# Other hand-written orders of each engine's work in a four-batch attention kernel

## What is computed

```
def _L0_xattn_ref(x, weight):             # x: layernorm(x), weight: ctx
    xq = quant_dequant_act_1x128(x)       # fp8, one scale per row and 128 columns
    wq = quant_dequant_weight_128x128(weight)   # fp8, one scale per 128x128 block
    return einsum('emk,enk->emn', xq, wq)

def _L0_ffn_ref(x, Wa, Wp, w_std, w_rec):
    fused = x @ (Wa * col_scale)
    Qf, Kf, V = ...                       # 16 heads of 32
    scores = einsum('bhtd,bhsd->bhts', Qf, Kf) / sqrt(32)
    attn = softmax(where(causal, scores, min))
    y = einsum('bhts,bhsd->bhtd', attn, V)
    return y.reshape(Bx, Tx, C) @ Wp

x = x + tanh(g_xattn) * _L0_xattn_ref(_layernorm(x), ctx)
x = x + tanh(g_ffn) * _L0_ffn_ref(_layernorm(x), Wa, Wp, w_std, w_rec)
```

## Time and profile before

| | us |
|---|---|
| median of three runs | 499.98 (499.82 to 503.68) |
| the profiled execution | 499.74 |
| its span, first to last instruction | 497.9 |
| around the span | 1.84 |

### The profile page before, as it was taken

One profiled execution on the slowest core, in us unless ns is written; L12 is line 12 of the kernel. 1 busy time (PEld: TensorE's weight loads), 2 busy tenths in 40 slices (PEclk: granted clock), 3 DMA queues, 4 the chain that ended last, 5 costly groups with the idle time before them and its releaser, 6 DMA issues.

```text
span 497.9 us, 7913 instructions
## 1 busy us (share of the span) xinstructions
PE 440.6 (88%) x2536; PEld 317.1 (64%) x2536; DVE 340.3 (68%) x1122; ACT 255.7 (51%) x498; POOL 151.1 (30%) x278
## 2 busy tenths in 40 slices
PE   0375989998979999998969999999879999999996
PEld 0352767775536788775535788776545788776764
DVE  5999627889994254889995253789995246556633
ACT  1695356566646450667645642466654424554530
POOL 5678474343225200343213400243122101121110
PEclk9998799999989999999999999999998999999999
DMA  7402173323500346223500234424400243234102
GB/s 225 197 1 87 39 246 82 91 69 96 146 2 2 89 101 193 67 56 95 141 27 0 64 97 127 138 53 98 97 11 2 58 102 97 64 95 102 60 21 86
DMA packets 27929, 42.62 MB, mean 86 GB/s; under 512 B 8272, under 2 KB 8528, under 8 KB 27888
## 3 DMA queue, kind: packets, MB, share of 16 engines
q1 hardware_dynamic: 25872, 41.18, 29.6%
q10 hardware_dynamic: 1824, 0.54, 0.6%
q0 software_dynamic: 192, 0.39, 0.3%
HBM read 12.59 MB, written 4.19 MB: 34 GB/s over the span
## 4 chain that ended last, share of the span: by engine, by line
PE 66%; DVE 24%; ACT 3%; issue 3%; DMA 2%; POOL 1%; SPq 0%; ACTq 0%; DVEq 0%; POOLq 0%
PE pv_bank L748 13%; DVE x_all L1201 10%; PE mm_bank L594 9%; PE mm_bank L595 8%; PE mm_bank L596 8%; PE exp_bank L734 6%; PE max_bank L717 5%; DVE max_bank L1230 5%; PE mm_bank L775 2%; PE mm_bank L777 2%; PE mm_bank L776 2%; PE turn_bank L610 2%; DVE bn L1208 2%; PE pv_bank L757 1%; DMA x_all<-in_x 1%
## 5 line engine op out<-in xcount | busy, mean ns | idle before, releaser
L1230 DVE CUSTOM_DVE_ANT_0 max_bank<-max_bank,causal 128x512 f32<-128x512 f32 (+3 forms) x256 | 121.0, 512 | 52.5 <-PE max_bank L717 52.0
L1002 ACT ACTIVATE work<-exp_bank 128x512 f32<-128x512 f32 (+1 forms) x192 | 94.9, 526 | 56.2 <-PE exp_bank L734 55.2
L512 POOL TENSOR_SCALAR_AFFINE_SELECT work<-work 128x384 f32<-128x384 f32 x64 | 33.4, 522 | 281.6 <-ACT work L1002 281.6
L748 PE MATMUL pv_bank<-work,v_aug 128*33 128x256 f32 (+3 forms) x512 | 78.9, 451 | 0.6 <-DVE work L1241 0.2
L734 PE MATMUL exp_bank<-q_stack,k_stack 97*128 97x512 f32 (+3 forms) x256 | 71.2, 341 | 7.6 <-ACT work L1002 6.5
L717 PE MATMUL max_bank<-k_stack,q_stack 96*128 96x512 f32 (+3 forms) x256 | 71.1, 338 | 2.4 <-DVE row_max L1230 1.8
L1201 DVE SCALAR_TENSOR_TENSOR x_all<-mm_bank,coef,x_all 128x128 f32<-128x128 f32 x224 | 61.5, 342 | 0.3
L748 PEld LDWEIGHTS pv_bank<-work,v_aug 128*33 128x33 f32 x512 | 29.7, 113 | 50.1 <-issue 42.1
L734 PEld LDWEIGHTS exp_bank<-q_stack,k_stack 97*128 97x128 f32 x256 | 45.6, 188 | 23.4 <-ACT work L1002 14.7
L594 PE MATMUL mm_bank<-xt_hi,w_hi 128*128 128x512 f32 x128 | 53.4, 417 | 0.7 <-ACT v_aug L981 0.7
L717 PEld LDWEIGHTS max_bank<-k_stack,q_stack 96*128 96x128 f32 x256 | 45.2, 191 | 12.7 <-DVE row_max L1230 3.7
(11 more groups left out here) (168 smaller groups left out, 789.1 us busy)
## 6 DMA issues: line engine op xcount, KB each, us to landing
q_stack<-qk_hi SPq DMA_DIRECT2D x128, 64.0 KB, 2.0
k_stack<-qk_hi SPq DMA_DIRECT2D x120, 64.0 KB, 2.0
x_all<-in_x SPq DMA_DIRECT2D x16, 256.0 KB, 3.6
ctx_raw<-in_ctx SPq DMA_DIRECT2D x16, 256.0 KB, 3.9
q_stack<-qk_lo SPq DMA_DIRECT2D x64, 64.0 KB, 2.0
out<-x_all SPq DMA_DIRECT2D x16, 256.0 KB, 2.4
k_stack<-qk_lo SPq DMA_DIRECT2D x60, 64.0 KB, 2.0
work<-in_L_ffn_Wa SPq DMA_DIRECT2D x3, 768.0 KB, 9.7
```

The costliest lines, as they stand in the source:

```text
L512: pool.affine_select(out=three, in_=three, compare_op=ALU.is_ge, fill=0.0, base=0, pattern=[[0, 3], [1, P]], channel_multiplier=-1)
L748: last = pe.matmul(pv_bank[64 * j:64 * j + D + 1, P * m:T], v_aug[:, m, 2 * u + j, :], prob[j][:, PROB_COL[m]:PROB_COL[m] + T - P * m], st ...
L1002: act.activation(prob[j][:, UNIT_COL[k]:UNIT_COL[k] + UNIT_LEN[k]], exp_bank[(3 * j + k) % 2][:, 0:UNIT_LEN[k]], ACT.Exp, scale=SCALE).the ...
L1230: last = dve.tensor_tensor_reduce(max_bank[unit % 2][:, col:col + width], max_bank[unit % 2][:, col:col + width], causal[:, T - width:T], ...
```

## The change

The strings are written anew for the eight steps of the middle batches (used by batches 0 to 2), for the last batch, for the prologue and for the end sections; nothing else is changed, neither an operation, nor a buffer, nor the table BEFORE. The block sums now stand as S0 to S6, S7 to S11, S12 to S15 in steps 3, 4 and 5 of DVE (before S0 to S4, S5 to S9, S10 to S15). The block maxima of ctx (t) stand in steps 4 and 5, all ahead of the last maxima of step 5. The quarters of q0, k0, q1, k1 are divided otherwise between step 7 and the end section. The norm stands behind back at the end of steps 3 to 5, and W, X, x, u, b and H pieces stand at other places.

```diff
--- before.py
+++ after.py
@@ -38,105 +38,105 @@
 
 
 PE_STEPS = [
-    "max0 max1 rowmax W0 Q2.0 max2 v3.012 exp0 max3 exp1 W1 exp2 Q2.1 exp3 max4 v3.3 exp4 max5 exp5",
-    "Q2.2 max0 max1 rowmax Q2.3 pv exp0 exp1 max2 max3 W2 K2.0 max4 exp2 K2.1 exp3 back K2.2 max5 exp4 exp5 W3",
-    "max0 K2.3 max1 rowmax Q3.0 pv exp0 Q3.1 max2 Q3.2 exp1 max3 max4 back exp2 Q3.3 K3.0 exp3 K3.1 exp4 K3.23 exp5 max5 X0",
-    "max0 rowmax max1 S0 S1 pv max2 S2 max3 X1 max4 exp0 S3 back S4 exp1 exp2 S5 S6 max5 X2 exp3 exp4 exp5",
-    "rowmax max0 max1 S7 pv max2 max3 S8 S9 exp0 max4 exp1 back exp2 exp3 exp4 max5 X3 exp5 S10",
-    "S11 max0 rowmax max1 pv S12 max2 S13 max3 H0 S14 exp0 exp1 max4 exp2 H1 exp3 exp4 S15 exp5 max5 back",
-    "max0 rowmax max1 A0 pv exp0 H2 max2 exp1 exp2 max3 max4 exp3 exp4 max5 exp5 back",
-    "A1 rowmax H3 pv q0.0 exp0 exp1 q0.12 back exp2 q0.3 k0.0 exp3 k0.123 exp4 q1.012 exp5 q1.3 k1.012",
+    "max0 max1 rowmax W0 Q2.0 v3.01 max2 exp0 exp1 max3 v3.2 max4 exp2 exp3 Q2.1 max5 v3.3 exp4 exp5",
+    "max0 max1 Q2.23 W1 rowmax pv K2.0 exp0 exp1 W2 max2 max3 back exp2 K2.1 exp3 exp4 max4 max5 K2.23 exp5",
+    "max0 rowmax Q3.0 max1 W3 pv Q3.12 exp0 exp1 Q3.3 max2 max3 K3.0 exp2 max4 exp3 K3.12 back exp4 exp5 K3.3 max5",
+    "X0 max0 rowmax max1 S0 S1 pv S2 S3 max2 max3 exp0 X1 max4 exp1 S4 exp2 S5 exp3 max5 exp4 exp5 back",
+    "X2 max0 S6 rowmax max1 S7 max2 pv S8 exp0 max3 exp1 S9 exp2 max4 exp3 S10 exp4 S11 X3 exp5 max5 back",
+    "max0 H0 rowmax S12 max1 pv S13 max2 exp0 exp1 max3 S14 exp2 max4 exp3 S15 exp4 H1 max5 exp5 back",
+    "max0 max1 A0 rowmax pv exp0 exp1 max2 H2 exp2 max3 exp3 max4 exp4 max5 exp5 back H3",
+    "rowmax A1 pv q0.01 exp0 q0.2 exp1 q0.3 exp2 k0.0 exp3 exp4 back k0.12 exp5 k0.3 q1.0",
 ]
 
 ACT_STEPS = [
-    "neg W0 exp0 exp1 exp2 W1 exp3 exp4 exp5 v3",
-    "neg Q2 exp0 exp1 copy exp2 W2 exp3 exp4 exp5",
-    "K2 neg W3 copy exp0 C0 exp1 Q3 exp2 exp3 exp4 K3 exp5 X0",
-    "neg C1 copy X1 C2 exp0 exp1 exp2 exp3 exp4 exp5",
-    "neg X2 copy C3 exp0 exp1 exp2 exp3 exp4 exp5",
-    "X3 neg N0 N1 H0 exp0 copy exp1 exp2 H1 exp3 exp4 exp5",
-    "neg N2 N3 exp0 H2 exp1 exp2 copy exp3 exp4 exp5",
-    "H3 neg exp0 copy exp1 c0 exp2 q0 exp3 k0 exp4 exp5 c1",
+    "neg W0 exp0 exp1 exp2 exp3 exp4 exp5 v3",
+    "Q2 neg W1 copy exp0 exp1 exp2 exp3 exp4 W2 exp5 K2",
+    "neg C0 exp0 copy exp1 Q3 exp2 W3 exp3 exp4 exp5 K3",
+    "X0 neg C1 C2 exp0 X1 copy exp1 exp2 exp3 X2 exp4 exp5",
+    "neg C3 exp0 exp1 exp2 exp3 copy N0 exp4 exp5 X3",
+    "H0 neg exp0 copy exp1 N1 exp2 exp3 exp4 exp5 H1",
+    "neg N2 N3 exp0 exp1 H2 exp2 exp3 copy exp4 exp5",
+    "H3 neg exp0 copy exp1 exp2 q0 exp3 exp4 c0 exp5",
 ]
 
 DVE_STEPS = [
-    "max0 max1 max2 max3 x0 x1 max4 max5 x2",
-    "x3 max0 max1 L0 Q2 max2 max3 m0 max4 L1 norm max5 L2",
-    "m1 L3 max0 e0 K2 max1 max2 m2 m3 e1 norm max3 max4 Q3 max5",
-    "K3 max0 max1 S0 S1 max2 max3 S2 S3 S4 norm max4 max5",
-    "b0 S5 max0 S6 S7 max1 b1 max2 S8 max3 max4 S9 norm max5",
-    "S10 max0 max1 S11 t0 S12 max2 max3 H0 S13 max4 S14 b2 S15 t1 t2 max5 t3 norm b3 H1",
-    "A0 max0 max1 max2 max3 max4 max5 H2 norm",
-    "H3 A1 norm q0 k0 q1",
+    "max0 max1 max2 max3 max4 x0 max5",
+    "x1 x2 x3 Q2 max0 max1 L0 m0 L1 max2 max3 m1 max4 max5 norm L2",
+    "e0 max0 K2 L3 max1 m2 m3 max2 max3 max4 Q3 e1 norm max5",
+    "K3 max0 S0 S1 max1 S2 max2 S3 max3 S4 max4 S5 norm max5 S6",
+    "max0 max1 b0 S7 max2 b1 S8 S9 max3 S10 max4 norm t0 max5 S11",
+    "H0 S12 max0 t1 max1 t2 t3 b2 max2 S13 S14 max3 max4 S15 max5 norm b3",
+    "A0 max0 max1 H1 max2 max3 H2 max4 max5 norm H3",
+    "A1 norm q0",
 ]
 
 POOL_STEPS = [
     "zero0 zero1 i0",
-    "zero0 zero1 u0 u1",
     "zero0 zero1",
-    "u2 u3 zero0 zero1",
-    "zero0 zero1 r0",
+    "u0 u1 zero0 u2 zero1",
+    "zero0 zero1 u3",
+    "r0 zero0 zero1",
     "zero0 zero1",
-    "r1 zero0 zero1 g0 g1",
-    "g2 g3 zero0 zero1",
+    "r1 zero0 zero1",
+    "g0 g1 zero0 g2 zero1 g3",
 ]
 
 PE_LAST = [
-    "max0 rowmax max1 Q2.01 v3.01 max2 exp0 exp1 v3.2 max3 exp2 max4 v3.3 exp3 exp4 Q2.2 max5 exp5",
-    "max0 Q2.3 rowmax K2.01 max1 max2 pv exp0 exp1 K2.23 max3 exp2 max4 exp3 back exp4 Q3.0 max5 exp5",
-    "max0 Q3.1 rowmax max1 max2 pv max3 exp0 exp1 Q3.2 back exp2 max4 exp3 Q3.3 exp4 max5 exp5 K3.0",
-    "max0 K3.1 rowmax max1 pv max2 exp0 max3 exp1 K3.2 exp2 back max4 exp3 K3.3 exp4 max5 exp5",
-    "Y0 max0 max1 rowmax Y1 pv exp0 max2 exp1 max3 z0 Y2 exp2 exp3 back exp4 max4 exp5 max5 Y3",
-    "max0 rowmax max1 pv max2 exp0 exp1 max3 max4 back exp2 exp3 max5 z1 exp4 exp5",
-    "Y4 rowmax max0 max1 pv max2 max3 exp0 exp1 Y5 exp2 max4 back max5 exp3 exp4 Y6 exp5 Z0",
-    "rowmax z2 pv exp0 exp1 Y7 exp2 exp3 back exp4 exp5",
+    "max0 max1 rowmax Q2.0 v3.01 Q2.1 max2 exp0 exp1 max3 v3.2 exp2 v3.3 exp3 max4 exp4 max5 Q2.2 exp5",
+    "Q2.3 rowmax K2.0 max0 max1 pv exp0 K2.1 exp1 max2 max3 exp2 K2.2 exp3 max4 K2.3 exp4 max5 exp5 Q3.0 back",
+    "rowmax max0 Q3.1 max1 pv exp0 max2 exp1 max3 Q3.2 exp2 max4 back exp3 max5 exp4 Q3.3 exp5",
+    "K3.0 max0 rowmax K3.1 max1 pv max2 exp0 exp1 K3.2 max3 back exp2 max4 exp3 K3.3 exp4 max5 exp5",
+    "Y0 max0 rowmax z0 max1 pv exp0 exp1 Y1 exp2 max2 max3 back exp3 exp4 max4 Y2 max5 exp5",
+    "Y3 rowmax max0 max1 pv max2 exp0 max3 exp1 z1 back exp2 exp3 max4 max5 exp4 exp5 Y4",
+    "rowmax max0 max1 pv max2 exp0 max3 exp1 Y5 exp2 exp3 max4 max5 back exp4 exp5",
+    "Y6 rowmax Z0 pv exp0 exp1 Y7 exp2 exp3 z2 back exp4 exp5 Z1",
 ]
 
 ACT_LAST = [
-    "neg exp0 exp1 exp2 exp3 exp4 v3 exp5",
-    "Q2 neg exp0 exp1 copy exp2 exp3 K2 exp4 exp5",
-    "neg copy exp0 exp1 exp2 exp3 exp4 exp5 Q3",
-    "neg copy exp0 exp1 exp2 exp3 exp4 K3 exp5",
-    "neg copy exp0 z0 exp1 exp2 exp3 exp4 exp5",
-    "neg copy exp0 exp1 exp2 exp3 exp4 exp5",
-    "neg z1 exp0 exp1 copy exp2 exp3 exp4 exp5",
-    "neg copy exp0 exp1 exp2 exp3 exp4 z2 exp5",
+    "neg exp0 exp1 exp2 exp3 exp4 v3 exp5 Q2",
+    "neg exp0 copy exp1 exp2 exp3 exp4 exp5",
+    "K2 neg exp0 copy exp1 exp2 exp3 exp4 exp5",
+    "neg Q3 copy exp0 exp1 exp2 exp3 K3 exp4 exp5",
+    "neg copy exp0 exp1 z0 exp2 exp3 exp4 exp5",
+    "neg copy exp0 exp1 exp2 exp3 exp4 exp5 z1",
+    "neg exp0 exp1 copy exp2 exp3 exp4 exp5",
+    "neg exp0 exp1 copy exp2 exp3 exp4 exp5",
 ]
 
 DVE_LAST = [
     "max0 max1 max2 max3 max4 max5",
-    "max0 Q2 max1 max2 max3 max4 norm max5",
-    "max0 K2 max1 max2 max3 norm max4 max5",
-    "max0 max1 max2 max3 Q3 max4 norm max5 K3",
-    "Y1 max0 max1 max2 max3 z0 norm max4 max5",
-    "max0 max1 Y3 max2 max3 norm max4 max5",
-    "max0 max1 max2 max3 Y5 z1 max4 max5 norm Y7 Z0",
-    "norm",
+    "Q2 max0 max1 max2 max3 max4 max5 norm K2",
+    "max0 max1 max2 max3 max4 max5 norm",
+    "max0 max1 max2 Q3 max3 max4 max5 norm K3",
+    "max0 max1 max2 max3 max4 max5 norm",
+    "max0 max1 z0 max2 Y1 max3 norm max4 max5",
+    "Y3 max0 max1 max2 max3 z1 Y5 max4 max5 norm",
+    "Y7 Z0 norm",
 ]
 
-PE_FIRST = ("f0 f1 f2 f3 f4 S0 S1 S2 S3 f5 S4 S5 S6 f6 S7 S8 f7 S9 f8 S10 S11 S12 S13 S14 "
+PE_FIRST = ("f0 f1 f2 f3 f4 S0 S1 S2 f5 S3 S4 S5 S6 f6 S7 S8 S9 f7 S10 S11 S12 f8 S13 S14 "
      "S15 f9 f10 v0 f11 v1 q0 B0 B1 k0 V2 q1 M0 k1 M1 M2")
 
-ACT_FIRST = ("a0 C0 C1 C2 f0 d0 f1 C3 f2 C4 b0 f3 f4 C5 C6 f5 a1 C7 f6 b1 f7 N0 f8 a2 "
-     "a3 N1 f9 N2 b2 f10 N3 b3 v0 f11 v1 q0 k0 c0 V2 D0 c1 p0 q1 D1 k1 c2 c3")
-
-DVE_FIRST = ("x0 w0 x1 x2 x3 t0 t1 L0 L1 t2 t3 L2 A0 A1 T0 F0 F1 L3 F2 F3 T1 T2 c0 S0 "
-     "S1 S2 S3 b0 S4 S5 S6 S7 S8 b1 S9 S10 S11 S12 b2 S13 h0 S14 S15 b3 T3 h1 u0 u1 "
-     "h2 u2 h3 u3 B0 q0 B1 k0 M0 q1 M1 M2 k1")
-
-POOL_FIRST = ("i0 s0 s1 s2 s3 s4 s5 o0 s6 j0 s7 r0 j1 l0 l1 r1 l2 l3 r2 r3 j2 j3 g0 g1 "
+ACT_FIRST = ("a0 C0 d0 C1 C2 f0 C3 f1 C4 f2 f3 f4 C5 a1 f5 C6 C7 b0 b1 f6 N0 a2 f7 a3 "
+     "b2 f8 N1 N2 f9 b3 N3 v0 f10 f11 q0 p0 k0 v1 c0 V2 D0 c1 q1 D1 c2 k1 c3")
+
+DVE_FIRST = ("x0 x1 x2 x3 w0 t0 t1 L0 t2 t3 L1 A0 T0 A1 F0 T1 F1 L2 L3 F2 F3 c0 T2 S0 "
+     "S1 S2 S3 S4 S5 b0 S6 S7 S8 b1 S9 S10 T3 S11 b2 S12 h0 S13 S14 S15 b3 u0 h1 h2 "
+     "u1 h3 u2 u3 B0 B1 q0 k0 q1 M0 M1 M2 k1")
+
+POOL_FIRST = ("i0 s0 s1 s2 s3 s4 s5 s6 l0 s7 l1 r0 o0 j0 r1 j1 l2 r2 l3 r3 j2 j3 g0 g1 "
      "D0 g2 D1 g3 p0")
 
-PE_END = "pv k1.3 V0.012 max0 back V0.3 max1 V1.01 y0 max2 y1 V1.2 max3 V1.3 V2.0 max4 V2.123 max5 y2 y3 O0 O1 O2 O3"
-
-ACT_END = "q1 k1 copy V0 y0 V1 y1 c2 V2 y2 c3 y3"
-
-DVE_END = "k1 norm max0 max1 max2 max3 y0 max4 y1 max5 y2 O0 y3 O1 O2 O3"
+PE_END = "q1.123 k1 pv V0.01 max0 back V0.23 y0 V1.0 max1 V1.1 max2 V1.2 max3 V1.3 y1 max4 V2 max5 y2 y3 O0 O1 O2 O3"
+
+ACT_END = "k0 c1 q1 c2 copy k1 y0 c3 V0 V1 y1 V2 y2 y3"
+
+DVE_END = "k0 q1 k1 norm max0 max1 y0 max2 max3 max4 y1 max5 y2 y3 O0 O1 O2 O3"
 
 END_LAST = {
-    "PE": "Z1 Z2 pv Z3 back Z4 Z5 z3 Z6 Z7 Z8 Z9 Z10 Z11",
-    "ACT": "copy z3",
-    "DVE": "z2 Z1 Z2 norm Z3 z3 Z8 Z9 Z10 Z11",
+    "PE": "Z2 pv Z3 back Z4 Z5 z3 Z6 Z7 Z8 Z9 Z10 Z11",
+    "ACT": "z2 copy z3",
```

(1 more changed line is left out.)

## The result

The changed kernel takes 504.79 us (median of 19 runs, 502.63 to 508.07), the kernel before 500.70 beside it (19 runs). The ratio of the runs is 1.0064, with a 95% interval of 1.0049 to 1.0079: slower by about 3.2 us. The sign and the range held. The reasons held only in part, and the main term was not in the sum. The time lies at the lower end of what the forecast gave to another cause (norms that wait for back, 503 to 508, chance .22), which did not happen.

A forecast was written before the change was run, and what follows sets the result against it. A batch was taken as PE-bound, then DVE-bound for 34 us, then PE-bound again. Terms: 499.74 - 2.9 (stretch) + 1.2 (clock) + .75 (scales) + 2.0 (step 0) = 500.79, median 501.0 us; range 495.5 to 506.

The forecast's parts named there:

- The sign and the range: Whole kernel: forecast 1.0 us slower than before, in a range of 495.5 to 506 us.
- norms that wait for back: Rival, ends of steps 3 to 5: back ends late, DVE's norm waits, time 503 to 508 us; chance .22.
- The stretch, K3 to turn(6): From K3 to step 6's turn of row maxima: DVE's work sums to 34.6 us, from 34.02 before.
- the step on the load of ctx: t0, moved up into step 4: load lands in time as stacking ends about two us earlier; 0, bounds 0 and 1.4.
- The clock: pv(6): PE's idle is spread, so the clock stays up in two of three batches; one falling costs +1.2 us.
- the term from turn(6) to exp0: End of the stretch, three batches: first scores of step 6 come earlier, mainly from faster pv(6); gain 2.9 us.
- Scales in step 2: e1's coefficient operations slow beside GpSimd's u2 multiplication; +.25 us a batch, +.75 in three.
- Step 0: Start of each batch: v3's quarter moves behind exp0, PE waits for the negative maxima's DMA; .65 to .7 each, +2.0 us.
- Prologue and last batch: First and last parts of the kernel: pieces only change places, gains and losses cancel; 0, bounds -1 and +1 each.
- End of the batches: Six q and k quarters move to the end section; k0's stacking still lands before the next maxima; 0, bounds 0 and 1.0.
- The sum: Whole kernel: 499.74 - 2.9 + 1.2 + .75 + 2.0 = 500.79 us, as a median 501.0.
- exp0 to the next turn(0): From step 6's first scores to the next batch's first turn of row maxima: no change, 0.

The follow-up runs named there:

- experiment 1: Changed kernel with the first ctx block maximum (t0) moved back from step 4 to step 5: 1.0035 to the kernel before.
- experiment 2: Changed kernel with SP's load of ctx issued ahead of six stacking DMAs, t0 left in step 4: 1.0001 to the kernel before.
- experiment 8: experiment 2 with H3 back behind the turn of row maxima of step 7 and max3 ahead of exp2 in step 6: 1.0040 to the kernel before.
- experiment 9: experiment 2 with the quarter v3.2 back in front of exp0 in PE's step 0: 1.0046 to the kernel before.
- experiment 6: Kernel before with the last scores' matmul of step 5 done 16 times in batches 0 to 2, filling PE's idle: .9974 to the kernel before.
- experiment 3: Changed kernel with GpSimd's multiplication for u2 moved back from step 2 to step 3: 1.0059 to the kernel before.
- experiment 11: Kernel before with the 16 repeated matmuls of experiment 6 and the change's last-batch strings: .9955 to the kernel before, 499.07 us.
- experiment 4: Kernel before with only the change's prologue strings, on all four engines: 1.0024 to the kernel before.

## Why the prediction came out as it did

**The stretch, K3 to turn(6): the step on the load of ctx failed.** The forecast had 34.6 us, measured were 36.33 and 36.37 in batches 0 and 1. It put t0's wait at "0, bounds 0 and 1.4": the K2 half "ends a step earlier, so the 24 stacking DMAs ahead of it on SP end about two us earlier". PE and ScalarE do end K2 earlier, but the low half of K2 on DVE still stands behind e0 and max0 in step 2, and SP waits for that one. The stacking began at 221.32, K3 - 8.5 (before 217.09, K3 - 8.1), and ran on up to the load, 42 DMAs of about .63 us with less than 1 us of breaks. I followed the piece on two of its three engines. The waits, 1.36 and 1.46 us, came out at the upper bound that the forecast gave, and experiments 1 and 2 take them away. Without them DVE's sum was about right: turn(6) came at K3 + 34.5 to 35.2 in experiments 1, 2, 8 and 9. In batch 2, where no ctx maximum is, 32.4 was forecast and 32.06 measured.

**The clock: right, for a reason not quite right.** One slow pv(6) in three batches was forecast and is what the profile shows, and the term from turn(6) to exp0 is -4.4 us for -2.9. But in batch 1 it was not that PE's idle had become too small: the clock fell earlier, on pv(5), behind the idle that the wait for ctx made, and was back for pv(6). The wait for ctx is not needed for a fall: without it the clock fell in all three batches in experiment 1, all three pv(6) being slow, and in two of three in experiment 2, once early enough to be over. So how many of three are slow is luck of the execution as much as the order's doing: the changed kernel and its variants had seven fast pv(6) in 21, from 0 to 2 a profile. That PE's idle in front of pv(6) matters to the clock is shown by experiment 6 and the counts there. What the forecast missed is that the gain isn't kept: up to 1 us of each fast pv(6) goes back in the next stage, by the traces since ScalarE's norms hold the exponentials (+1.36 us in the table, forecast 0). The cover of an idle of PE was taken as gone once PE was fast, and ScalarE, which hangs on DVE's statistics and not on pv, was next.

**Scales in step 2.** Right in kind. The pair of operations took 1.17 us beside GpSimd:

```profile
227.78 1.17 DVE L1149 SCALAR_TENSOR_TENSOR coef<-x_down,gates,w_down 128x16 f32<-128x16 f32 x2
227.83 1.09 POOL L505 TENSOR_TENSOR tile_buf<-tile_buf,x_up 128x512 f32<-128x512 f32 x1 [1.17 <-DVE x_down L1125]
```

It costs .24 to .4 us a batch (experiment 3; forecast .25), and moving u2 away did not make the kernel faster. The pair ends with the multiplication (228.95 and 228.92 us), as the Trainium skill's lock ("SBUF — State Buffer", SBUF: two separate sides) has it.

**Step 0: the term was mis-sized, and its sign is wrong.** Forecast were .65 to .7 us a batch of waiting for the DMA of the negative maxima, "That DMA does not come sooner". In batch 0 of the profiled execution this was so: it was issued 1.4 us after the turn, as before, and exp0 came after 3.70 us (3.72 before) with .83 us of idle. In batches 1 and 2 it came sooner. The lines of batch 2, answering to the earlier trace rows:

```profile
315.18 0.27 PE L723 MATMUL exp_bank<-ident,row_max 128*8 128x128 f32 x1
...
317.40 1.73 SPq L443 DMA_DIRECT2D x_all<-in_x  x3
318.27 0.53 PEld L734 LDWEIGHTS exp_bank<-q_stack,k_stack 97*128 97x128 f32 x3 [0.24 <-DMA q_stack<-neg_max]
```

Exp0 comes after 3.09 us (before 3.82), in batch 1 after 3.24 (3.64). SP finishes the stacking of the next batch's k later, so the loads of x go out 2.2 us after the turn and not 1.3, and the row may land in front of them. That this is the reason isn't shown: in batch 1 of experiment 8 they went out 1.5 us after the turn and exp0 came after 2.99. By experiment 9 the quarter is better behind exp0, by .1 to .5 us. The stage became longer by .4 to 1.05 us all the same, in part by the step above and in batch 0 by the late DMA; the rest was not traced, and its total of +2.1 for +2.75 is partly luck.

**No wait for back.** The rival that had DVE wait for back at the ends of steps 3 to 5 did not happen: DVE has no idle in front of a norm there. Its outcome (some us slower) came by another wait on the same engine.

**Prologue and last batch.** Both were given 0 with bounds of 1 us. The prologue measured +1.09 to +1.2, just outside. The forecast looked at ScalarE's casts, the copy of v1 and the third ctx top; the traces point at two pieces that it did not name, GpSimd's r2 and DVE's T3. The last batch gave -.7 to -.85.

**End of the batches.** The forecast had the last stacking DMA land 2.6 us after its issue, 1.5 us before the next batch's first maxima; the trace of before has it 2.0 us on, so the slack was 2.1. The term of 0 held: no wait for k_stack is in PE's list after the change.

**The sum.** 501.0 was forecast and 504.79 measured, against 500.70 in the same runs: +1.0 for +3.2 to +4.1. The difference of 2 to 3 us is about the 2.8 us of the two waits for ctx. The other misses of the table (prologue +1.1, clock -1.5, exp0 to the next turn(0) +1.4, last batch -.7, turn(0) to K3 -.65) add up to -.4 us, which is luck.

## What to carry to other kernels

When a consumer moves earlier in a kernel with hand-written orders, follow its input to the queue that issues it, through each engine that the producers pass: here PE and ScalarE had moved and DVE had not, and SP's load did not come a microsecond earlier. A wait on the engine that is the bound is lost (1.36 and 1.46 us of DVE here, 1.45 and 1.19 at turn(6)), and idle of the other engine can cost too, where that is PE: its clock fell behind such idles. Before a gain is counted, ask who else the next piece waits for; here, by the trace, it was ScalarE behind two norms. And where a clock falls in one execution and not in the next, a single profile of each of two kernels is not enough to tell 1 us.

## What was not expected of the hardware

Sixteen repetitions of a matmul, 1.9 us of work that nobody needs, made the kernel faster by 1.3 us (.9974): the granted clock stayed at its upper level on pv(6) in two batches of three, for none before. Which batch falls differs from execution to execution: experiments 6 and 11 have the same strings up to the last batch, and pv(6) was slow in batch 1 of the one and in batch 0 of the other. A slow clock is not free wherever PE has idle: on pv(5) it cost nothing, on pv(4) DVE waited 1.10 and 1.17 us for the block sum behind it.

The mean clock of a run is a poor measure of this. These two rows are the same stretch of the prologue, first of the changed kernel, then of experiment 1, which has the same prologue (the clock is third from the end):

```profile
40.00:56.00 16.00, 10.25 (x36) 7.37 (x34) 14.45 (x49) 7.93 (x13) 13.91 (x23) 1.00 0.11 40
40.00:56.00 16.00, 10.24 (x36) 7.28 (x34) 14.36 (x49) 7.94 (x13) 13.91 (x23) 0.50 0.11 34
```

PE does the same 36 matmuls in the same time, at a clock said to be 1.00 and .50. From 28 to 45 us a block sum's matmul of 512 columns takes 628 to 796 ns in both, and 446 ns on average in the steps of the changed kernel, where the clock is 1.00 but for a few us; so the clock was low in the first as well, and its profile doesn't show it. The mean clocks of the two executions, .988 and .945, differ mostly by this. The times of the kernel before show it as well: beside the runs of experiments 1 to 4, those with a mean clock of .974 to .977 took 500.4 us in the median, those of .968 to .972 took 501.9, and the four of .957 to .961 took 501.0. What tells more than the mean is the time of a piece that every batch has, such as pv(6).
